# Moving the token normalisation of a macaron transformer block from GpSimd to VectorE

## The reference

```
x = x + 0.5 * ffn(layernorm(x))      # called A in the kernel
x = x + attention(layernorm(x))      # called B
x = x + 0.5 * ffn(layernorm(x))      # called C, same weights as A
layernorm(x) = (x - mean(x)) / sqrt(var(x) + 1e-5)
ffn(x)       = rms_norm(silu(x @ Wg) * (x @ Wu)) @ Wp     # ternary weights, hidden width 2048
attention: 32 heads of 16, blocks of 128 queries, keys of the same and the previous block
```

## Time and profile before

| | |
|---|---|
| device time, median of 3 (lowest to highest) | 2072.71 us (2071.61 to 2073.45) |
| the profiled execution's own time | 2072.0 us |
| its span, first to last instruction | 2070.1 us |
| PE / PEld busy | 1957.8 us (95%) / 1429.6 us (69%) |
| DVE busy | 1635.6 us (79%) |
| ACT busy | 1469.9 us (71%) |
| POOL busy | 803.2 us (39%) |
| mean granted TensorE clock | 0.981 |

### The profile page before, as it was taken

The page is one execution under the profiler, slowest core; times in us unless marked ns, Lnnn a source line. Parts: engine busy times, 40 slices in busy tenths (PEclk is TensorE's granted clock), DMA queues, the critical chain, the costliest instruction groups (busy, mean ns, idle before and its releaser), DMA issues. The chain is left out here.

```text
span 2070.1 us, 61748 instructions
## 1 busy us (share of the span) xinstructions
PE 1957.8 (95%) x24766; PEld 1429.6 (69%) x25022; DVE 1635.6 (79%) x4144; ACT 1469.9 (71%) x2617; POOL 803.2 (39%) x688
## 2 busy tenths in 40 slices
PE   6478899999999999999999999999999999999888
PEld 4356677777777777777777777777777777777566
DVE  7956888788877888778887888878887888878774
ACT  7746777677776777767776777777776777767772
POOL 1124334444444344434443444444444444443321
PEclk9779999999999999999999999999999999999999
DMA  6314775566664566656664666656655566746760
GB/s 212 130 31 85 126 106 111 96 110 111 122 119 86 103 111 114 114 88 118 121 112 85 105 115 119 108 93 116 117 97 101 105 114 118 119 80 104 130 114 27
DMA packets 760878, 222.23 MB, mean 107 GB/s; under 512 B 745744, under 2 KB 745744, under 8 KB 760080
## 3 DMA queue, kind: packets, MB, share of 16 engines
q1 hardware_dynamic: 760592, 218.26, 58.7%
HBM read 25.17 MB, written 8.39 MB: 16 GB/s over the span
## 5 line engine op out<-in xcount | busy, mean ns | idle before, releaser
L704 ACT ACTIVATE masked<-masked,exp_bias,exp_scale 128x256 f32<-128x256 f32 (+1 forms) x1024 | 503.8, 562 | 8.6
L1016 PEld LDWEIGHTS ps_gu<-xt_A,wgu_t 128*128 128x128 bf16 x8192 | 473.5, 99 | 38.0 <-DVE wgu_t L754 9.8
L1016 PE MATMUL ps_gu<-xt_A,wgu_t 128*128 128x128 f16 x8192 | 487.6, 221 | 12.4 <-DVE hid L836 6.0
L1016 PE MATMUL ps_gu<-xt_C,wgu_t 128*128 128x128 f16 x8192 | 482.6, 220 | 1.6 <-DMA xt_C<-xh 1.5
L1016 PEld LDWEIGHTS ps_gu<-xt_C,wgu_t 128*128 128x128 bf16 x8192 | 467.1, 98 | 11.6 <-DMA xt_C<-xh 1.6
L827 DVE TENSOR_TENSOR prob<-masked,prob 128x1024 f16<-128x1024 f32 (+1 forms) x256 | 354.4, 1384 | 7.1 <-ACT prob L727 7.1
L853 DVE CUSTOM_DVE_ANT_0 masked<-ps_s,mask 128x256 f32<-128x256 f32 (+1 forms) x1024 | 337.0, 384 | 0.0
L827 DVE TENSOR_TENSOR h_lo<-hid,h_hi 128x512 f16<-128x512 f32 x256 | 197.8, 773 | 130.9 <-ACT h_hi L592 130.0
L592 ACT ACTIVATE h_hi<-hid 128x512 f16<-128x512 f32 x256 | 160.3, 626 | 166.5 <-DVE hid L842 156.8
L561 POOL TENSOR_TENSOR acc_C<-acc_C,sq 128x512 f32<-128x512 f32 x95 | 121.0, 1274 | 380.6 <-ACT sq L721 380.6
L1074 PE MATMUL ps_yy<-wp_t,h_lo 128*128 128x512 bf16 x1024 | 264.5, 381 | 0.0
(11 more groups left out here) (163 smaller groups left out, 2262.6 us busy)
## 6 DMA issues: line engine op xcount, KB each, us to landing
stream<-in_L_attn_x_dram SPq DMA_DIRECT2D x32, 256.0 KB, 3.3
pt<-prob SPq DMA_TRANSPOSE x512, 3.2
out_dram<-stream SPq DMA_DIRECT2D x32, 256.0 KB, 2.5
stream<-in_L_ffn_w_gate_up_dram SPq DMA_DIRECT2D x4, 1024.0 KB, 5.4
prob<-in_L_ffn_w_gate_up_dram SPq DMA_DIRECT2D x4, 1024.0 KB, 5.6
stream<-in_L_ffn_w_proj_dram SPq DMA_DIRECT2D x2, 1024.0 KB, 5.8
prob<-in_L_ffn_w_proj_dram SPq DMA_DIRECT2D x2, 1024.0 KB, 6.2
wv<-in_L_attn_Wo_dram SPq DMA_DIRECT2D x1, 1024.0 KB, 7.8
```

The lines of the kernel that those rows point to most:

```text
L704: t = act.activation(p, p, ACT.Exp, bias=exp_bias[:, 4 * g + h:4 * g + h + 1], scale=exp_scale[:, 0:1])
L1016: t = pe.matmul(bank[:, j * P:(j + 1) * P], wgu_t[:, k, at:at + P], xt[s][:, part, k, :], start=(k == 0 and part == 0), stop=(k == KD - 1 ...
```

## The change

In the steps, `norm_apply` leaves GpSimd: `xhat_free` and the tensor_scalar into xhat go to VectorE, in the same step, between `normalise_o` and `gated`. VectorE waits for the factor (g_rstd) there. GpSimd keeps `power` and `low`. The instruction signals the same semaphore g_xh. This concerns 93 instructions: 30 blocks of A, 32 of B, 31 of C.

```
@@ gpsimd, step_of @@
                     if b is not None and in_steps(s, b):
                         power(rstd[s], var_eps[s], d_ve[s], g_rstd[s], b)
-                        xhat_free(pool, step)
-                        norm_apply(s, b)
@@ vector, step_of @@
                     add_output(LAST)
                     norm_stats("C", LAST, d_x2, NB)

+                for s, offset in (("B", XHAT_B), ("C", XHAT_C), ("A", XHAT_A)):
+                    b = block_at(step, offset)
+                    if b is not None and in_steps(s, b):
+                        dve.wait_ge(g_rstd[s], b + 1)
+                        xhat_free(dve, step)
+                        dve.tensor_scalar(xhat[:, :], slot(b), mean_var[s][:, 0:1], rstd[s][:, 0:1],
+                                          ALU.subtract, ALU.mult).then_inc(g_xh[s], 1)
+
                 s, bf, c, n = gate_at(step)
                 if s and not (s == "A" and bf == 0):
                     gated(s, bf, c, n)
```

## The result

The changed kernel takes 2075.8 us in the median of 12 runs (2074.88 to 2079.6), the kernel before 2072.54 us in 12 (2068.89 to 2074.16). The medians are 3.3 us (0.16%) apart; the ratio on record, worked out from all the runs, is 1.0021 with a 95% interval of 1.0013 to 1.0028. The time lies within the forecast band of 2070.5 to 2076, at its upper end, and the interval leaves out 1: the changed kernel is slower by a little, and that little is clear of the noise. The profiled execution has a span of 2072.6 us (2070.1 before) at the same mean granted clock of 0.981.

The account below looks back on a forecast made before the run. TensorE sets the pace, waiting for late VectorE in twenty blocks. Terms -1.8 + 0.1 + 0.7 + 0.9 + 0.6 = +0.5 on 2072.0, with 0.7 for the median, predict 2073.2 us; forecast band 2070.5 to 2076 (0.56), 8 in 10: 2069.5 to 2083.

Parts of the forecast that it names:

- What bounds it: TensorE sets the pace; in twenty blocks it waits for VectorE at step 7's gate, 0.26 us a block lost.
- The price: Each moved instruction holds up what is behind it on VectorE by 0.47 us, bounds 0.41 to 0.54.
- Step 1: C's instruction, 31 times: costs nothing, vanishing in VectorE's 2.4 us wait for the keys.
- Step 3: A's instruction, 30 times: no wait for the factor, and the shift ends in VectorE's idle time in step 4.
- The gift of step 4: Step 3's shift puts prob ahead of GpSimd's low part of A, giving VectorE 0.53 us back until step 6.
- Step 6 in full blocks: B's instruction in 13 late blocks: gate 6 to gate 7 takes 6.25 us instead of 6.39, -1.8 us together.
- rival 1: Step 4's gift doesn't come, 0.47 us paid in twenty blocks: 2084; one case has prob starting before the fold. Chance 0.18.
- The seven half-size blocks: Late blocks beside a half-size prob: 0.45 us back by the same order against 0.47 paid, +0.1 us for the seven.
- Head and tail: First factor of B before Wo +0.7; spread quarters +0.9 for B and +0.6 for C and A.
- 2: Order holds in part of the blocks, or the instruction takes 0.54 and meets GpSimd's sums in step 6: 2079. Chance 0.12.
- rival 3: Faster: the new instruction is free in step 6 and the 0.26 a block comes back in twenty blocks: 2070. Chance 0.10.
- rival 4: Faster: GpSimd's tensor_scalar locks out VectorE's two-input instructions, so removing it speeds up step 6: net 2070. Chance 0.04.

Follow-up runs that it names:

- e3: Kernel before, nothing moved; GpSimd's low part of A in step 4 waits until VectorE's low part of the probabilities is done: 2067.1 us, ratio 0.9981.
- e2: Only B's normalised tokens (step 6) moved to VectorE, A and C left on GpSimd as in the kernel before: 2083.7 us, ratio 1.0054.
- e7: A's and C's normalised tokens moved to VectorE, B left on GpSimd as in the kernel before: 2069.3 us, ratio 0.9984.
- e1: Only A's normalised tokens (step 3) moved to VectorE, B and C left on GpSimd as in the kernel before: 2070.2 us, ratio 0.9988.
- e5: Changed kernel, with GpSimd's low part of A in step 4 waiting until o_norm of that step is written: 2072.6 us, ratio 1.0001.
- e8: Kernel before, all tokens on GpSimd, with its low part of A in step 4 waiting until o_norm is written: 2068.2 us, ratio 0.9981.
- e6: Changed kernel, with B's normalised tokens behind the gated product of step 6 instead of in front of it: 2069.3 us, ratio 0.9989.
- e4: Changed kernel, with GpSimd's low part of A in step 4 waiting until VectorE's low part of the probabilities is done: 2077.7 us, ratio 1.0025.
- e9: Changed kernel, with GpSimd's sum of C's squares in step 6 waiting for VectorE's h_lo of step 5: 2069.0 us, ratio 0.9982.
- e10: Kernel before, nothing moved; low parts of A (step 4) and C (step 2) wait for o_norm, sum of C's squares for step 5's h_lo: 2066.3 us, ratio 0.9970.

## Why the prediction was right, and where it was off

The time came out in the forecast band, and the mechanism (a price in step 6, a gift in step 4, TensorE waiting at the gate of step 7) is what the traces show. But "no change that can be told" was too strong: 24 runs do tell a slowdown of 0.1 to 0.3%. The sum was 2.6 us short by the medians and 2.0 by the two spans, and its errors partly cancelled: the half-size blocks cost 3.1 more than reckoned and the full ones gave 0.5 less, head and tail cost 1.4 less, and the stretches between the blocks gave 0.3. With head and tail as I had them the kernel would have stood near 2077.2, outside the band, so that it stayed inside is in part luck.

- **What bounds it** (VectorE late at the gate of step 7 in twenty blocks, up to 0.26 each to be had): right. e3 takes just that 0.26 in full blocks and 0.12 in half-size ones, and ends at 6.13, the floor that I took from the earlier block.
- **The price**, 0.47: right. 0.54 busy, 0.46 to the next start; e2 pays 0.44 to 0.47 a block.
- **Step 1**, nothing: right, e7 against e1. The wait for the keys fell from 75.2 to 66.6 us in its 32 places of the whole run, 0.27 each and not 0.47.
- **Step 3, no loss at once**: right in full blocks.
- **The gift of step 4**, 0.53: right, v to the gated product is 3.00 (3.02 predicted, 3.55 before). e3 proves its cause, since there nothing is moved but the order.
- **Step 6 in full blocks**: 6.25 predicted, 6.28 measured. With four blocks touched by stalls the thirteen give -1.3 instead of -1.8. One of the four, the block whose gate 7 stands at 987.02 before, is rival 1's other case. A stall in step 3 makes the fold 0.36 later still; now prob starts before the fold, and the fold and the low part come behind it and run into o_norm (1.04 instead of 0.63):

```profile
970.96 1.22 DVE L825 TENSOR_TENSOR prob<-masked,prob 128x1024 f16<-128x1024 f32 x1
...
972.71 1.04 DVE L866 TENSOR_TENSOR o_norm<-o_sum,row_inv 128x128 f32<-128x128 f32 x1
```

```profile
971.09 1.40 POOL L568 TENSOR_TENSOR acc_A<-acc_A 128x128 f32<-128x128 f32 x1
```

  Gate 6 to gate 7 is 6.61 there. The same happens in the changed kernel in the very block from which I took the good state: prob starts at 256.44, the fold at 256.59, o_norm takes 1.04, and the block needs 6.75 instead of 6.13. I had counted it among those with reserve.
- **The seven half-size blocks**: this step failed, +0.1 predicted, +3.2 measured. I said that there too the order would turn and 0.45 come back. I had read the step from one block, at 1141 us, and it was not typical. In a typical one the kernel before has on GpSimd

```profile
908.51 0.46 POOL L568 TENSOR_TENSOR acc_A<-acc_A 128x128 f32<-128x128 f32 x1
910.00 1.16 POOL L525 TENSOR_TENSOR xh<-xhat,xh 128x512 f16<-128x512 f32 x1 [1.03 <-ACT xh L592]
```

  so the low part waits for ScalarE 1.03 us after the fold. The shift of step 3 (VectorE's instruction waits 0.44 for the factor and the gated product comes 0.98 later in its step) uses that reserve up (910.36 + 0.46 against 910.86 in the changed kernel) and stops just short of turning the order. The block at 1141 us was untypical because VectorE had stalled by 0.36 in front of it (last section): its low part waits only 0.69 for ScalarE, where the other six wait 1.03 to 1.05, and with 0.69 my sum would have turned the order. And e5 shows that even with the order turned only 0.28 of the 0.46 would have come back, because of the shorter prob_v and because VectorE then waits for TensorE in step 5.
- **Head and tail**, +2.2: too much. The wait for Wo is 3.08 us instead of 2.62:

```profile
134.96 5.36 PE L1022 MATMUL ps_gu<-xt_A,wgu_t 128*128 128x128 f16 x64 [3.08 <-DVE wo L809]
```

  That is +0.46 for +0.7, and the spread blocks paid less than I gave them: 0.32 us to the gate at 273.73 and 0.47 behind the last late block. How much of the head is the change's stays open: the gate that stands at 255.11 before stands between 253.05 (e8) and 258.02 (e6) in the others, in both directions.
- **Rivals.** 1 (the gift fails everywhere, 2084) is what e2 measures, 2083.7, and needs A to stay on GpSimd; its case of prob before the fold occurs twice in the changed kernel, as shown above. 2 had the right order of size, in a part of the blocks, for a reason it named: "the order holds in a part". 3's 2070 is what e1, e6 and e7 reach, not by a cheaper instruction but where the price falls outside TensorE's wait. 4 is refuted by e2. The Trainium skill ("SBUF — State Buffer", section "Who interferes with whom") has a GpSimd instruction that reads SBUF and a VectorE instruction with two SBUF inputs exclude each other. For GpSimd's two-input instructions all runs agree: prob 2.19 or 1.22, o_norm 0.84 or 0.29, h_lo 1.43 or 0.68, by nothing but what GpSimd did beside them. For its tensor_scalar the prediction judged from one place, and neither "disturbed nobody" (rival 3) nor "not for the tensor_scalar" (rival 4) holds in general: it excludes VectorE too, but only in its first 0.6 us or so (last section), and not for the whole of it. In the late blocks prob of step 6 starts 0.72 behind it, so e2 could take it away and not a tenth of a microsecond came back.

## What to carry to other kernels

Before moving work off an idle engine, ask what its instructions do to the busy one: here the 190 us less on GpSimd weren't what gained anything, and a wait that let one low part start 1.3 us later was worth 5. A new instruction in a full queue costs its time only if it stands between the last late input and the result that the bounding engine waits for; behind that result it was free. And when a term is counted for several blocks, read two or three of them first, since one block with a stall in it is enough to turn a margin of 0.05 us around on paper.

## What the runs showed of the hardware

**GpSimd's tensor_scalar keeps VectorE out only at its start.** In the seven blocks whose probabilities in step 6 are half-size, prob starts 0.18 us behind it and takes 1.12 us:

```profile
389.58 2.08 POOL L520 TENSOR_SCALAR xhat<-stream,mean_var_B,rstd_B 128x512 f32<-128x512 f32 x1 [0.18 <-POOL rstd_B L516]
```

```profile
389.76 1.12 DVE L827 TENSOR_TENSOR prob<-masked,prob 128x512 f16<-128x512 f32 x1
```

It takes 1.12 or 1.13 in all seven of the kernel before, e1, e3, e7 and e8, where B's tokens are on GpSimd, and 0.68 in all seven of the changed kernel, e2, e4, e5 and e6, where they are not. (In e9 and e10 the moved sum of C's squares runs beside it, and it takes 1.19 or 1.20.) So prob was held up by 0.44 us, that is until some 0.6 us of the 2.08 had passed (an estimate from these rows, and lengths on GpSimd are rough), and one that starts 0.72 inside isn't held up at all (1.21). The other way round GpSimd waits: in step 3, where a full-size prob runs when A's instruction is issued, it takes 2.63 instead of 2.08.

```profile
309.51 1.22 DVE L827 TENSOR_TENSOR prob<-masked,prob 128x1024 f16<-128x1024 f32 x1
```

```profile
310.05 2.63 POOL L520 TENSOR_SCALAR xhat<-stream,mean_var_A,rstd_A 128x512 f32<-128x512 f32 x1 [0.18 <-POOL rstd_A L516]
```

None of it is in the device time: gate 6 to gate 7 of those seven blocks is 5.82 or 5.83 in every kernel, since VectorE has reserve there.

**A low part issued early ends sooner than one that waits on a semaphore.** A low part that is issued while prob runs ends 1.02 us after prob; one that waits for prob's semaphore ends 1.25 after it (e4).

**VectorE stalls by 0.36 us at fixed places of its program.** In the kernel before, four instructions of VectorE start some 0.36 us late for no reason that the profile names; in the changed kernel four others do. One of each:

```profile
1136.33 0.29 DVE L868 TENSOR_TENSOR o_norm<-o_sum,row_inv 128x128 f32<-128x128 f32 x1 [0.44 <-issue]
```

```profile
563.99 0.75 DVE L840 SCALAR_TENSOR_TENSOR hid<-ps_gu,h_scale_u,hid 128x512 f32<-128x512 f32 x1 [0.56 <-DVE hid L834]
```

(the second wait usually shows 0.21). They are no accident of one execution. e3, with VectorE's program of the kernel before, has them at the same four instructions; e4 and e9, with that of the changed kernel, have them at the other four, each 18 gated products behind the last (e8 and e10 show three of the first four, e6 all of the second four, e5 three of them). So an instruction added to a queue also moves such places; what makes them isn't shown here. Where TensorE waits for VectorE and one falls into steps 3 to 6, it is paid (two full blocks before, two after, of which the one at 966.85 by turning the order of step 4); with slack in step 6, as in e9 and e10, every late block stayed at 6.13. The first row stands one step ahead of the rows from which I read the half-size blocks, and made VectorE late in them.

**One projection in the tail runs at two speeds.** The 12 matmuls for V of the last block take 2.75 us in eight of the twelve kernels and about 4.4 in e1, e3, e8 and e9, one profiled execution each. The windows over them, before and in e8 (the last but two numbers are the granted clock):

```profile
1966.38:1968.97 2.59, 2.59 (x14) 1.17 (x14) 1.61 (x9) 1.27 (x2) 0.56 (x1) 1.00 0.67 128
```

```profile
1958.78:1963.06 4.28, 4.28 (x14) 1.61 (x14) 1.61 (x9) 1.27 (x2) 0.56 (x1) 0.60 0.69 132
```

The granted clock has a mean of 0.60 there, so a good part of the stretch ran at the lower of its two levels, 1.2 GHz. In front of it TensorE had been idle for 1.40 + 0.20 + 0.45 + 0.66 us in the kernel before and 1.41 + 0.20 + 0.23 + 0.88 in e8, 2.7 both times. That is 1.7 us in the total which no edit explains (whether one kernel shows both speeds in different executions was not looked at), and a reason to compare steady stretches rather than single medians.
